# A cross-attention layer with MLP on one core: the first norm's scale and shift folded into q's weights and bias, v's bias into the output bias

## The reference

```python
x = layer_norm(hidden_states, ln1_w, ln1_b)
q = x @ q_w + q_b;  k = ctx @ k_w + k_b;  v = ctx @ v_w + v_b     # 16 heads of 32
attn = softmax(where(mask, q k^T / sqrt(32), min))
hidden = (attn v) @ cproj_w + cproj_b + residual
y = layer_norm(hidden, ln2_w, ln2_b)
out = hidden + gelu(y @ fc_w + fc_b) @ proj_w + proj_b
```

## Time and profile before

| | us |
|---|---|
| median of 3 runs | 763.83 (758.85 to 768.42) |
| the profiled execution | 762.24, span 760.4 |
| TensorE busy | 700.5 (92%) |
| VectorE busy | 464.7 (61%) |
| ScalarE busy | 321.7 (42%) |
| GpSimd busy | 251.7 (33%) |

### The profile page before, as it was taken

How to read it: one execution, slowest core, us unless ns; L and a number is a source line. 1 busy time by engine, 2 the same in 40 slices (tenths; PEclk the granted TensorE clock), 3 DMA queues, 4 the chain that set the end, 5 groups by cost and what they waited for, 6 DMA issues and landing times.

```text
span 760.4 us, 13145 instructions
## 1 busy us (share of the span) xinstructions
PE 700.5 (92%) x4544; PEld 607.7 (80%) x4544; DVE 464.7 (61%) x860; ACT 321.7 (42%) x581; POOL 251.7 (33%) x217
## 2 busy tenths in 40 slices
PE   2789989899999989899689999999999999999998
PEld 2678879798888979798567888888888888888886
DVE  5567978978888888978858675432225233251213
ACT  4337766767676676857652211112211121211110
POOL 3505556655646656656653111000000001000000
PEclk9888989999999999999889999999999999999999
DMA  9655654644555554444604400010001000010001
GB/s 249 209 168 142 169 163 127 174 114 149 147 167 140 154 157 123 112 129 141 181 1 149 142 1 1 1 55 1 1 0 56 0 0 0 0 55 1 1 0 57
DMA packets 51130, 69.16 MB, mean 91 GB/s; under 512 B 8328, under 2 KB 29192, under 8 KB 51088
## 3 DMA queue, kind: packets, MB, share of 16 engines
q1 hardware_dynamic: 50816, 68.07, 30.9%
q0 software_dynamic: 272, 0.54, 0.3%
HBM read 47.21 MB, written 20.99 MB: 90 GB/s over the span
## 4 chain that ended last, share of the span: by engine, by line
PE 71%; issue 9%; DVE 8%; POOL 6%; DMA 3%; ACT 2%; SPq 0%; DVEq 0%; ACTq 0%; POOLq 0%
PE psum L1172 8%; PE psum L1174 8%; PE psum L1173 8%; PE psum L1159 8%; PE psum L1158 8%; PE psum L1157 8%; PE psum L975 5%; PE psum L976 5%; PE psum L977 5%; POOL p_lo L462 5%; PE psum L1059 3%; PE psum L1009 2%; PE psum L993 2%; DVE negm L731 2%; DVE xn L833 1%
## 5 line engine op out<-in xcount | busy, mean ns | idle before, releaser
L462 POOL TENSOR_TENSOR p_lo<-p,p_hi 128x512 f16<-128x512 f32 x128 | 157.1, 1236 | 135.6 <-ACT p_hi L535 135.1
L662 ACT ACTIVATE h<-psum,cols 128x512 f32<-128x512 f32 x64 | 44.1, 690 | 290.1 <-PE psum L1159 290.0
L913 DVE CAST h_hi<-h 128x512 fp32r<-128x512 f32 x64 | 27.6, 431 | 207.4 <-ACT h L662 207.4
L533 ACT ACTIVATE p<-psum,maskbias 128x512 f32<-128x512 f32 x128 | 88.3, 690 | 44.8 <-PE psum L993 42.7
L1172 PE MATMUL psum<-w_mlp,h_hi 128*128 128x512 f32 x256 | 100.8, 394 | 0.9 <-DVE hidden L758 0.9
L1174 PE MATMUL psum<-w_mlp,h_lo 128*128 128x512 f32 x256 | 99.7, 390 | 0.0
L1173 PE MATMUL psum<-w_mlp,h_hi 128*128 128x512 f32 x256 | 99.7, 389 | 0.0
L1157 PE MATMUL psum<-y_hi,w_mlp 128*128 128x512 f32 x256 | 99.7, 389 | 0.0
L1159 PE MATMUL psum<-y_hi,w_mlp 128*128 128x512 f32 x256 | 99.6, 389 | 0.0
L1158 PE MATMUL psum<-y_lo,w_mlp 128*128 128x512 f32 x256 | 99.6, 389 | 0.0
L535 ACT ACTIVATE p_hi<-psum,maskbias 128x512 f16<-128x512 f32 x128 | 88.7, 693 | 0.0
(11 more groups left out here) (104 smaller groups left out, 1511.3 us busy)
## 6 DMA issues: line engine op xcount, KB each, us to landing
qk_rows<-qk SPq DMA_DIRECT2D x32, 512.0 KB, 2.7
stacks<-qk_rows SPq DMA_DIRECT2D x64, 256.0 KB
stacks<-qk_rows SPq DMA_DIRECT2D x64, 128.0 KB
hidden<-in_x_dram SPq DMA_DIRECT2D x8, 512.0 KB, 4.4
ctx_sb<-in_ctx_dram SPq DMA_DIRECT2D x8, 512.0 KB, 5.1
w_mlp_raw<-in_L_xattn_fc_w_dram SPq DMA_DIRECT2D x16, 256.0 KB, 4.6
w_mlp_raw<-in_L_xattn_proj_w_dram SPq DMA_DIRECT2D x16, 256.0 KB, 6.3
out_dram<-hidden SPq DMA_DIRECT2D x16, 256.0 KB, 2.1
```

The source lines that it names most:

```text
L462: pool.tensor_tensor(p_lo[:, slot, :], p32[:, u % 2, :], p_hi[:, slot, :], ALU.subtract).then_inc(s["p_lo_done"], 1)
L533: act.activation(p32[:, u % 2, :], psum[:, ST + kc, :], ACT.Exp, bias=maskbias[:, kc:kc + 1], scale=SCALE32)
```

## The change

- **q's weights.** ScalarE's high part of each of the four column pieces is made in four instructions of 128 columns with ln1_w as the scale, VectorE's low part likewise (multiply, then subtract the high part). k's part is as before. The pieces 2 and 3 and the output weights' high part are made one or two steps later than before; the output weights' low part on GpSimd moves to step (-1, 3).
- **q's bias.** Four fp32 matmuls of one column per piece (fold_norm_bias) compute ln1_b @ Q, and VectorE adds it to the bias.
- **x.** Its transposes move from g = 3 for two batches ahead to g = 0 for the next batch; high and low parts are made in two halves straight from PSUM. affine_x and x_t are gone. Both groups of context transposes now come ahead of values.
- **v.** v1 is cast half by half straight from PSUM in g = 1 and 2; add_values becomes PSUM minus v1. The subtraction at the end of g = 3 is gone.
- **Output bias.** v's bias is repeated over the partitions in two parts, and 12 matmuls in step (0, 0) with an addition give the folded bias. GpSimd adds it to hidden in g = 3 instead of g = 1.

```diff
-        USES = [("qk", 0), ("ctx", 0), ("ctx", 1), ("m", 0), ("c", 1),
+        USES = [("qk", 0), ("ctx", 0), ("ctx", 1), ("x", 0), ("x", 1), ("m", 0), ("c", 1),
                 ("qk", 1), ("m", 1), ("att", 0), ("att", 1), ("v", 0),
                 ("qk", 2), ("m", 2), ("v", 1),
-                ("qk", 3), ("m", 3), ("c", 0), ("x", 0), ("x", 1)]
+                ("qk", 3), ("m", 3), ("c", 0)]
...
-                if g == 1 and batch(it + 1):
-                    b = it + 1
+                if isinstance(it, int) and (it, g) == (-1, 3):
+                    split_weight_lo(3)
+                if g == 3 and batch(it):
+                    b = it
                     wait(pool, "x_normed", (b + 1) * 2)
-                    wait(pool, "small_loaded", SMALL)
+                    wait(pool, "cb_folded", 1)
...
-                for n in range(2):
-                    act.activation(w_att[:, n, 0, :, c * P:(c + 1) * P], w_att_raw[:, n, 1, :, c * P:(c + 1) * P],
-                                   ACT.Copy).then_inc(s["w_hi_qk"], 1)
+                for k in range(KT):
+                    act.activation(w_att[:, 0, 0, k, c * P:(c + 1) * P], w_att_raw[:, 0, 1, k, c * P:(c + 1) * P],
+                                   ACT.Copy, scale=cols[:, LN1W + k:LN1W + k + 1]).then_inc(s["w_hi_qk"], 1)
+                act.activation(w_att[:, 1, 0, :, c * P:(c + 1) * P], w_att_raw[:, 1, 1, :, c * P:(c + 1) * P],
+                               ACT.Copy).then_inc(s["w_hi_qk"], 1)
...
+            def first_part(it, t):
+                b = it + 1
+                if isinstance(b, int) and b == 0:
+                    wait(act, "mask_stored", 16)
+                wait(act, "v_added", b * 2)
                 wait(act, "v_cast", b * 2)
+                wait(act, "v_proj", b * 2 + (t + 1))
+                act.activation(v1[:, t, :], in_bank("v", t), ACT.Copy).then_inc(s["v1_cast"], 1)
...
+            def x_hi(it, j):
+
+                b = it + 1
+                wait(act, "x_tr", b * 2 + (j + 1))
+                act.activation(xs[:, 0, 2 * j:2 * j + 2, :], in_bank("x", j).rearrange("p (k q) -> p k q", k=2),
+                               ACT.Copy).then_inc(s["x_hi_done"], 1)
...
                 if g == 0:
                     if batch(it + 1):
                         context_hi(it, 0)
+                        context_hi(it, 1)
                     exps(it, g, 0)
                     if batch(it + 1):
-                        context_hi(it, 1)
+                        x_hi(it, 0)
+                        x_hi(it, 1)
                     exps(it, g, 1)
                     maxima_out(it, g)
-                    if batch(it + 1) and not (isinstance(it, int) and it == -1):
-                        x_hi(it + 1)
...
-                if g == 3 and batch(it + 2):
-                    affine_x(it + 2)
+                if g in (1, 2) and batch(it + 1):
+                    first_part(it, g - 1)
                 exps(it, g, 2)
                 exps(it, g, 3)
                 if g == 0 and batch(it):
                     values_cast(it, 0)
-                if g == 2 and batch(it + 1):
-                    first_part(it + 1)
...
             def qk_weights_lo(c):
...
+                dve.wait_ge(s["qb_mm"], c + 1)
...
+                dve.tensor_tensor(cols[:, QB + c:QB + c + 1], cols[:, QB + c:QB + c + 1], psum[:, ST, 2 * c:2 * c + 1],
+                                  ALU.add).then_inc(s["qb_folded"], 1)
+                dve.wait_ge(s["w_hi_qk"], (KT + 1) * (c + 1))
+                for k in range(KT):
+                    piece = w_att[:, 0, :, k, c * P:(c + 1) * P]
+                    dve.scalar_tensor_tensor(out=piece[:, 1], in0=w_att_raw[:, 0, 1, k, c * P:(c + 1) * P],
+                                             scalar=cols[:, LN1W + k:LN1W + k + 1], in1=piece[:, 0].bitcast(fp32),
+                                             op0=ALU.mult, op1=ALU.subtract).then_inc(s["w_lo_dve"], 1)
...
             def add_values(it, t):
                 b = it + 1
-                wait(dve, "v_proj", b * 2 + (t + 1))
+                wait(dve, "v1_cast", b * 2 + (t + 1))
                 wait(dve, "v_split", b)
-                dve.tensor_tensor(v32[:, t, :], in_bank("v", t), vb_bc[:, :], ALU.add).then_inc(s["v_added"], 1)
+                dve.tensor_tensor(v32[:, t, :], in_bank("v", t), v1[:, t, :], ALU.subtract).then_inc(s["v_added"], 1)
...
             def step(it, g):
                 low_parts(it, g)
+                if isinstance(it, int) and it == -1 and g > 0:
+                    qk_weights_lo(g)
...
                 if g == 0 and batch(it + 1):
-                    context_lo(it, 0)
-                    context_lo(it, 1)
+                    for j in range(2):
+                        context_lo(it, j)
+                    for j in range(2):
+                        x_lo(it, j)
...
-                if g == 0 and batch(it + 1) and not (isinstance(it, int) and it == -1):
-                    x_lo(it + 1)
...
-                if g == 3 and batch(it + 2):
-                    affine_x(it + 2)
...
-                if g == 3 and batch(it + 1):
-                    wait(dve, "v1_cast", it + 2)
-                    dve.tensor_tensor(v32[:, :, :], v32[:, :, :], v1[:, :, :], ALU.subtract).then_inc(s["v_rest"], 1)
...
+            def fold_norm_bias(c):
+
+                pe.wait_ge(wqk_loaded[c], 32)
+                pe.wait_ge(s["ln1_loaded"], 32)
+                for k in range(KT):
+                    ins = nc.tensor.matmul(psum[:, ST, 2 * c:2 * c + 1], w_att_raw[:, 0, 1, k, c * P:(c + 1) * P],
+                                           cols[:, LN1B + k:LN1B + k + 1], start=(k == 0), stop=(k == KT - 1))
+                ins.then_inc(s["qb_mm"], 1)
+
+            def fold_value_bias():
+
+                pe.wait_ge(s["vb_lo"], 1)
+                pe.wait_ge(s["w_lo_pool"], 1)
+                three_passes(psum[:, PV + 1, :], [(vb_rep[:, 0, k, :], vb_rep[:, 1, k, :], w_att[:, 3, 0, k, :], w_att[:, 3, 1, k, :])
+                                                  for k in range(KT)]).then_inc(s["fold_mm"], 1)
...
                 if g == 0:
-                    transposes(it, "ctx", 0, it + 1, ctx_sb, "ctx_loaded", 16, "ctx_tr")
+                    for j in range(2):
+                        transposes(it, "ctx", j, it + 1, ctx_sb, "ctx_loaded", 16, "ctx_tr")
+                    if isinstance(it, int) and it == -1:
+                        fold_norm_bias(0)
                     values(it, g)
-                    transposes(it, "ctx", 1, it + 1, ctx_sb, "ctx_loaded", 16, "ctx_tr")
+                    for j in range(2):
+                        transposes(it, "x", j, it + 1, xn, "x_normed", 2, "x_tr")
+                    if isinstance(it, int) and it == 0:
+                        fold_value_bias()
                     scores(it, g, (0, 1))
                     transpose_max(it, g)
...
-                    transposes(it, "x", 0, it + 2, xn, "x_normed", 2, "x_tr")
...
-                if g == 3:
-                    transposes(it, "x", 1, it + 2, xn, "x_normed", 2, "x_tr")
```

113 lines of the change are left out of this document (48 added, 65 removed).

## The result

The changed kernel takes **776.5 us** (median, 775.28 to 777.24) against 762.65 us for the kernel before (758.85 to 768.42): ratio 1.0154, 95% interval 1.0110 to 1.0197. So it is slower by 13.9 us, at the upper edge of my range, and not the level result that I forecast. Timed once more it gave 1.0162 (1.0131 to 1.0193).

What follows compares the result with a forecast made beforehand. TensorE, busy 700.5 of 760.4 us, was taken as the bound. 762.2 + 2.4 (batches) + 0 (start) + 2.0 (value bias) - 3 (clock) - 1 (end) = 762.6, so 763 us, no change; range 750 to 777.

Steps and rivals of the forecast that it cites:

- The second half of ctx: Group 0 of each batch: both ctx transpose groups now follow at once, so TensorE waits for VectorE's qk, +1.16 us.
- the 1.7 us wait for m: Group 1's maxima transposes: TensorE's wait for VectorE's m is all but gone, maxima at 278.8 instead of 279.53, -0.7 us.
- Groups 1 and 2: v1's cast on ScalarE ahead of the exponentials delays p_lo and m: +0.2 us in each of the two groups.
- the stacks: Scores after group 1's maxima: SyncE's fills issued at 273.8 instead of 272.87; scores 0.9 us late by the bound, or no loss.
- The clock's term: Stretches of TensorE at 1.2 GHz: about 6 us of them go as the 1.7 us wait splits, -3 us (-8 to +10).
- the start: Up to the second batch's first projection at 49.2 us: both kernels level, 0, bounds -2 and +3.
- The small matmuls for the q bias: At the start: 16 fp32 matmuls, 1.6 to 9.3 us, taken at 0.1 each, under waits for stacks and VectorE.
- the value bias at +2.0 us: First batch's group 0: 12 matmuls of 2.84 us on TensorE, partly hidden by its waits there, +2.0 us.
- the end at −1 us: End of the batches: v's rest no longer stands ahead of the last q,k low part on VectorE, -1 us.
- The second: Rival, chance 0.15: group 0's waits along the bank chain bring the clock to 1.2 GHz, +10, late stacks +4: 777 us.
- The first: Rival, chance 0.15: VectorE was the real limit; its 0.8 and 1.7 us waits go and the clock holds: 748 us.
- The two rules weighed: Skill rules: PSUM reads dearer, some 1.4 us more per batch, set aside for the rows; four fp32 passes, 6.4 us.

Runs made afterwards that it cites:

- e1: Changed kernel, with SyncE issuing the stack fills ahead of the copy of the maxima, not behind it: ratio 1.0117 to the kernel before.
- e9: Kernel before, with GpSimd's three MLP column loads issued earlier, the low part of the output weights moved to step (-1,3): ratio 0.9996.
- e7: Changed kernel, with GpSimd's three MLP column loads issued later, behind the low part of the output weights: ratio 1.0130 to the kernel before.
- e2: Changed kernel, with the value bias's 12 matmuls behind the scores and the maxima's transposes of step (0,0): ratio 1.0084 to the kernel before.
- e4: Changed kernel, with GpSimd adding the output bias to hidden in group 1 again, not group 3: ratio 1.0102 to the kernel before.
- e14: The changed kernel itself, unaltered, timed again: ratio 1.0162 to the kernel before.
- e3: Changed kernel, with the second half of the ctx transposes behind the values matmuls again, its high part behind two exponentials: ratio 1.0157 to the kernel before.
- v's part alone: Kernel before with only the changes to v and the output bias: ratio 1.0043 in the first order (e5), 1.0042 in the mended order (e12).
- the mended order: Changed kernel: value bias matmuls behind maxima, column loads later, group 0 fills first, output bias in group 1 except batches 0 and 1: 1.0001 to the kernel before.
- e5: Kernel before with v1 cast from PSUM, v's bias folded by 12 matmuls, output bias added in group 3: ratio 1.0043.
- e12: Kernel before with v's part alone, its matmuls behind the maxima's transposes, output bias in group 1, group 0 fills first: ratio 1.0042.
- e16: The mended order, the last quarter's weights' low parts one group earlier, v's cast behind the third exponentials in groups 1 and 2: 1.0137 to the kernel before.

## Why the prediction was wrong

**Right, step by step.** The second half of ctx was to wait 1.16 us for VectorE's qk (1.0 measured), the maxima 0.61 us for x's low part (0.60), the output projection 0.46 us (0.22); the 1.7 us wait for m was to vanish and the maxima of group 1 to come 0.7 us earlier in the batch: they do, 23.04 us after the frame's start against 23.72. Groups 1 and 2 were to take 0.2 us more each. By the maxima's transposes it is 9.21 us against 9.02 from group 2 to 3, as said, but 11.08 against 9.99 from group 1 to 2: 1.1 us, with the wait for stacks in it. The batch was put at 42.5 to 43.5 us: 43.33.

**Mis-sized in the batch: the stacks.** I took the stack wait as 0, with +0.9 as the bound. It is 0.70 to 0.8 us in a steady batch, and a batch took +0.6 us instead of +0.4. e1 shows why this mattered little: behind it stood the wait I had named, for the low parts of the next q,k. Of the 0.6 us only 0.1 are in the waits listed; TensorE is busy 0.7 us longer in a batch (40.50 for 39.78) with the same matmuls, and no run shows why.

**The clock's term** of −3 us, for the 1.7 us wait being split, came true in the middle: six batches at +0.6 make +3.6, and the stretch of 289 us grew by 0.5. Between 115 and 370 us the changed kernel has no stretch at 1.2 GHz, the kernel before had four of 3.4 us, from 149.7, 323.8, 357.9 and 364.8 on. I did not foresee that the start and the end would take most of it back: over the whole trace it is 41 us at 1.2 GHz instead of 44.

**Failed: the start.** "By the first projection of the second batch at 49.2 both kernels are level: 0" was +3.8 us (53.03 against 49.24), beyond the 3 us that I had set as the mark of an error. The first projection of all was to start at 16.2 us and started at 17.82 (before: 18.32). I counted VectorE's and ScalarE's work there, but of what moved on GpSimd I counted nothing. With the low part of the output weights moved out, three column loads went from 31.0 us to 12.7 us, beside the last weights and ahead of the mask that SyncE waits for. e9 shows 2 us of it and e7 3.3, both at the first maxima. The small matmuls for the q bias, put under waits, stood in the open once, 0.7 us ahead of those maxima.

**Failed: the value bias at +2.0 us.** I priced its 12 matmuls right (2.82 us) and took a part off for cover. At that place there is none: the matmuls stand ahead of the maxima that begin a chain of 8.4 us to the next stacks. Moving them behind the maxima gives 5.4 us by the times and 3.9 by the traces (e2). The general error is that I worked out the steady batch and applied its slack to the first.

**Failed: the end at −1 us.** It was +3.2. I put the addition on GpSimd at 0, "behind the last p_lo, where GpSimd waits for the next batch's exponentials anyway", which holds in a steady batch and not in the last, where VectorE splits y for the MLP at that moment. e4 gives 4 us by the times, and the traces 2.6 on the mean. In sum: for the start and the value bias together I had +2.0 us and it was +10.2, for the end -1 and it was +3.2, and for the batches and their clock -0.6 and it was +0.5.

**The rivals.** The second gave nearly the right number, 777, for a reason that did not hold: in this trace no group 0 of the batches 1 to 7 had the clock fall (in e14's one had), and e3 took that wait away for nothing. It is luck that its number came near. The first did not come: VectorE has 10 us less to do and its two waits went, but new waits for it stood in their place.

**The two rules weighed.** The low parts of x from PSUM take 686 ns for 512 elements, beside the 0.68 us of the earlier trace rows; from SBUF it was 1596 ns for 1024. The Trainium skill (VectorE: DVE Perf Modes, Rules for kernel authors) gives the choice for elementwise work on a matmul's output: accept the slow rate of PSUM, or copy to SBUF first if many operations follow. That these subtractions would be dearer from PSUM than from SBUF was my reading of it and not its words, and the trace has no such price: the two halves take 1.37 us together, against 1.60 for the one that they replace and 1.22 for one of that size undisturbed. The small matmuls for the q bias, in the second row below, are 32 rows for 16 matmuls and 4.6 us busy, of which one group of four took 1.71 us at 1.2 GHz and the others 0.95:

```profile
L798 DVE TENSOR_TENSOR xs<-psum,xs 128x512 fp32r<-128x512 f32 x6 | 3.9, 686 | 2.9 <-ACT xs L592 2.9
```

```profile
L1105 PE MATMUL psum<-cols,w_att_raw 128*128 128x1 f32 x32 | 4.6, 263 | 0.0
```

I took 1.6 us. By the four passes of the Trainium skill (FP8 and Floating Point Precision, TensorE Precision Notes) the estimate was 6.4 us; the measured value lies between, nearer to that estimate, and with two records for each matmul the trace doesn't show how many passes there are. Three of the four groups ran under other waits, as forecast; the fourth is the one ahead of the first maxima.

**Still open.** Of the 6.2 us between the first two maxima the fold (2.8), the longer wait for VectorE (1.5) and x's wait in the bank chain (0.9) make 5.2. For the rest there is no experiment; TensorE was at 1.2 GHz for 6.8 us there (49.9 to 56.7) and for 3.4 us before (47.3 to 50.7), which can cost up to 1.7 us more. Of the 3.4 us at the first maxima no run parts the loads from the longer stretch at 1.2 GHz. The first maxima differ by 1.4 us between traces with the same loads and the same order, so single traces of the start are read to 1 or 2 us at most. And why v's part alone stays 3 us above the kernel before in the mended order, when the whole is level in it, is open.

## What to carry to other kernels

Work out the first and the last pass through a loop separately: an operation at zero cost in the steady state has its cover from neighbours that the first and last pass do not have. Ask of an added operation not how long it is but what chain starts behind it; the same 2.8 us of matmuls cost 4 to 5 us more in front of the instruction that starts a chain through DMA than behind it. And when one thing is moved out of an engine's queue, all behind it moves up: list those too. Last, cut a part out of the change only with a look at what it then stands beside: v's part alone had an operation of 5.11 us that the whole has not.

## What the runs showed of the hardware

The wait of 1.7 us on TensorE was followed by a stretch of 3.4 us at 1.2 GHz in two of the steady batches of the kernel before, but in all four from 190 us on in e5, in e9 and in e12, where the wait is the same. A group then takes 11.6 to 11.8 us instead of 10.0 to 10.2. With the wait cut into pieces of 1.0, 0.6 and 0.7 us (after) or left at 1.4 (e16) there was none. The 27 groups of the middle took 288.7 us before and 291.1, 292.8 and 293.7 us in e9, e12 and e5, so kernels with the same wait there differ by 2 to 5 us with the clock as the difference that the traces show. The spread of the kernel before (754.5 to 770.8 us in all) is larger still. Over 98 of its executions the time goes with the granted clock (0.01 less is about 4 us more, correlation -0.63), which fits; that the clock is the cause was not tried.
